# Graph attention with residual and layer norm: whole tiles of keys and queries in turns of two and one, scale found ahead of DVE's copies, ends reordered

## The reference

```
q = x @ Wq.T          k = x @ Wk.T          v = x @ Wv.T + bv
scores = einsum(q, k) * 384**-0.5 + 2 * adj          # per head, 128 x 128
scores = where(any(scores != 0 in the row), scores, -inf)
p = nan_to_num(softmax(scores))
out = einsum(p, v) @ Wo.T + bo
result = layernorm(x + out)
```

## Time and profile before

| | us |
|---|---|
| median of 3 runs | 605.71 |
| lowest and highest | 602.56, 606.85 |
| the profiled execution | 605.91 |
| its span | 604.1 |
| PE busy | 581.2 (96%) |
| ACT busy | 497.4 (82%) |
| DVE busy | 492.9 (82%) |
| POOL busy | 425.2 (70%) |
| mean granted clock of TensorE | 0.996 |

### The profile page before, as it was taken

One profiled execution on the slowest core, in us unless ns is written; L12 is line 12 of the kernel. 1 busy time (PEld: TensorE's weight loads), 2 busy tenths in 40 slices (PEclk: granted clock), 3 DMA queues, 4 the chain that ended last, 5 costly groups with the idle time before them and its releaser, 6 DMA issues.

```text
span 604.1 us, 23413 instructions
## 1 busy us (share of the span) xinstructions
PE 581.2 (96%) x8448; PEld 511.6 (85%) x8448; DVE 492.9 (82%) x2380; ACT 497.4 (82%) x1975; POOL 425.2 (70%) x691
## 2 busy tenths in 40 slices
PE   8889999999999999999999999999999999999776
PEld 5678888889988988888888988988888888898665
DVE  4568888888888888878887887888888888888886
ACT  5598888888887988978888887988988888887883
POOL 0476867867776876867867776876867777665763
PEclk9899999999999999999999999999999999999999
DMA  8401422414242241432323242241423231222221
GB/s 298 164 17 37 131 92 67 141 60 126 92 129 87 70 131 57 139 90 88 113 69 118 91 131 90 65 135 53 142 91 104 91 92 53 84 91 81 89 83 67
DMA packets 34748, 59.62 MB, mean 99 GB/s; under 512 B 10568, under 2 KB 24008, under 8 KB 34632
## 3 DMA queue, kind: packets, MB, share of 16 engines
q1 hardware_dynamic: 34200, 57.53, 30.0%
q10 hardware_dynamic: 432, 0.59, 0.3%
HBM read 44.50 MB, written 13.62 MB: 96 GB/s over the span
## 4 chain that ended last, share of the span: by engine, by line
PE 69%; DMA 11%; ACT 9%; DVE 4%; SPq 1%; issue 1%; POOL 0%; POOLq 0%; DVEq 0%
PE qk_ps L343 25%; PE scores_ps L441 12%; PE v_ps L379 11%; PE scores_ps L366 7%; ACT probs L491 7%; PE scores_ps L424 6%; PE qk_ps L396 6%; DMA scale_mem<-scale_rows 6%; DMA scale_t<-scale_mem 6%; DVE nscores L591 2%; DVE att_n L661 1%; ACT out_n L530 1%; SPq L252 1%; PE spare_ps L396 1%; SPq L248 0%
## 5 line engine op out<-in xcount | busy, mean ns | idle before, releaser
L491 ACT ACTIVATE probs<-nscores,neg_max 128x128 f32<-128x128 f32 x768 | 297.4, 389 | 13.3 <-DVE neg_max L591 9.0
L591 DVE CUSTOM_DVE_ANT_0 nscores<-scores_ps,adj_n 128x128 f32<-128x128 f32 x768 | 171.4, 285 | 29.1 <-PE scores_ps L366 27.1
L289 POOL TENSOR_TENSOR tree<-nscores 128x256 f32<-128x256 f32 x192 | 144.0, 750 | 18.9 <-DVE neg_max L591 18.9
L491 ACT ACTIVATION_READ_ACCUMULATOR probs<-nscores,neg_max 128x1 f32 x768 | 144.2, 188 | 0.0
L517 ACT ACTIVATE probs_t<-qk_ps 128x384 f32<-128x384 f32 (+1 forms) x128 | 63.1, 493 | 77.4 <-PE spare_ps L396 74.4
L441 PE MATMUL scores_ps<-w_o,att_t 128*128 128x384 f32 x576 | 112.3, 339 | 5.4 <-DVE probs_t L616 4.9
L379 PE MATMUL v_ps<-w_v,x_t 128*128 128x384 f32 x576 | 111.4, 338 | 3.5 <-ACT probs_t L517 3.5
L289 POOL TENSOR_TENSOR tree<-tree 128x128 f32<-128x128 f32 x192 | 101.3, 527 | 15.0
L379 PEld LDWEIGHTS v_ps<-w_v,x_t 128*128 128x128 f32 x576 | 101.7, 188 | 9.7 <-ACT probs_t L517 4.3
L343 PE MATMUL qk_ps<-x_t,w_q 128*128 128x512 f32 (+1 forms) x540 | 107.2, 343 | 0.7 <-ACT probs_t L517 0.7
L343 PE MATMUL qk_ps<-x_t,w_k 128*128 128x512 f32 (+1 forms) x540 | 107.8, 344 | 0.0
(11 more groups left out here) (71 smaller groups left out, 946.9 us busy)
## 6 DMA issues: line engine op xcount, KB each, us to landing
x_n<-xn SPq DMA_DIRECT2D x32, 384.0 KB, 5.1
scale_t<-scale_mem SPq DMA_DIRECT2D x63, 192.0 KB
out<-out_n SPq DMA_DIRECT2D x31, 384.0 KB, 2.6
x_raw<-xt SPq DMA_DIRECT2D x15, 768.0 KB, 5.5
adj_n<-adj SPq DMA_DIRECT2D x32, 128.0 KB, 4.6
scale_mem<-scale_rows SPq DMA_DIRECT2D x63, 16.0 KB
x_raw<-xt SPq DMA_DIRECT2D x3, 256.0 KB, 6.0
nscores<-wq ACTq DMA_DIRECT2D x3, 192.0 KB, 4.1
```

The source lines that it names most:

```text
L289: nc.gpsimd.tensor_tensor(tree[:, b % 2, low:high, 0:width], src[:, :, 0:width], src[:, :, width:2 * width], ALU.add).then_inc(tree_step, 1)
L491: last = nc.scalar.activation(probs[:, b % 2, h], nscores[:, b % 2, h], ACT.Exp, bias=neg_max[:, b % 2, h:h + 1], scale=-1.0, accum_out=ro ...
L591: last = nc.vector.tensor_tensor_reduce(out=nscores[:, half, h], in0=scores_ps[j][:, m * P:(m + 1) * P], in1=adj_n[:, b // 2 % 2, half], s ...
```

## The change

Tiles: `projected(b)` gives two whole tiles in even slots and one in odd slots. The second of the two goes to `qk_ps[1]` with 512 columns and is copied by ACT as a whole; in odd slots ACT copies nothing. Semaphore values follow (`second_tiles`).

DVE: `find_scale(b + 1)` comes right behind the biases and ahead of `keep_turned_high`, `keep_first` and `keep_v`.

PE: `project_out` waits for the biases of graph b + 2 (as the argument counts, `biased >= KT * (b + 4)`) in place of the copy `turned_high`. `attend` waits for `turned_high` always, and for ACT's copies in slots with fewer than two tiles.

Start: the low part of w_o moves on DVE from before the copies of the first queries into slot -2, and its high part on ACT behind the copies of the first keys; `softmax_top` of graphs 0 and 1 waits for the split weights, whose raw form lies in the same buffers.

End: POOL adds the bias rows of graphs 62 and 63 in slot 61; ACT copies the bank of `v_ps` first in the last two turns.

```
         def projected(b):
             ...
             if b % 2 == 0:
-                return (tile, 0, GRP * P), (tile + 1, 0, GRP * P // 2)
-            return (tile + 2, 0, GRP * P), (tile + 1, GRP * P // 2, GRP * P)
+                return tile, tile + 1
+            return (tile + 2,)
+
+        def second_tiles(b):
+            return (slots_with_tiles(b) + 1) // 2
# POOL
-                if has(b):
+                if 0 <= b < NB - 2:
                     add_bias(b)
+                if b == NB - 3:
+                    add_bias(NB - 2)
+                    add_bias(NB - 1)
# PE
             def project(b, n, tile):
                 ...
                 elif b == -1:
-                    pe.wait_ge((kept_first, kept_second)[n], 1)
+                    pe.wait_ge(kept_first, 1)
                 ...
-                        last = nc.tensor.matmul(qk_ps[n][:, start:end], w[:, a, k, cols], x_t[:, g % XBUFS, c, k, start:end],
+                        last = nc.tensor.matmul(qk_ps[n][:], w[:, a, k, cols], x_t[:, g % XBUFS, c, k],
             def values(b):
-                    pe.wait_ge(turned_low, LOWS * (b - 1) + 2)
+                    pe.wait_ge(turned_low, LOWS * (b - 1) + (2 if has(b + 1) else 1))
             def turn(b):
-                if b == 0:
-                    pe.wait_ge(kept_second, slots_with_tiles(b - 1))
-                elif not projected(b - 1):
+                if projected(b - 1):
+                    pe.wait_ge(kept_second, second_tiles(b - 1))
+                else:
                     pe.wait_ge(probs_ready, KT * (b + 1))
             def attend(b):
-                if projected(b):
-                    pe.wait_ge(kept_second, slots_with_tiles(b))
-                    if b == 0:
-                        pe.wait_ge(turned_high, 1)
-                else:
+                pe.wait_ge(turned_high, b + 1)
+                if len(projected(b)) < 2:
                     pe.wait_ge(turned_low, LOWS * (b + 1))
-                    pe.wait_ge(turned_high, b + 1)
             def project_out(b):
                 if has(b + 3):
-                    pe.wait_ge(turned_high, b + 2)
+                    pe.wait_ge(biased, KT * (b + 4))
# ACT
             def softmax_top(b, m):
                 ...
+                    if b < 2:
+                        act.wait_ge(w_split, b + 1)
             def keep_second(b):
-                act.wait_ge(proj_done, 2 * b + 6)
+                act.wait_ge(proj_done, tile + 1)
                 ...
-                nc.scalar.activation(dst[:, g % 2, t % KT, start:end], qk_ps[1][:, start:end], ACT.Copy,
-                                     scale=scale).then_inc(kept_second, 1)
+                nc.scalar.activation(dst[:, g % 2, t % KT], qk_ps[1][:], ACT.Copy, scale=scale).then_inc(kept_second, 1)
             ...
-            act.wait_ge(wo_in, DMA)
-            nc.scalar.activation(w_o[:, HI], raw_o, ACT.Copy).then_inc(w_high, 1)
             for m in range(KT):
                 act.wait_ge(first_done, 2 * m + 1)
                 nc.scalar.activation(k_t[:, 0, m], first_ps[2 * m][:], ACT.Copy).then_inc(first_keys, 1)
-            act.wait_ge(w_split, 2)
+            act.wait_ge(wo_in, DMA)
+            nc.scalar.activation(w_o[:, HI], raw_o, ACT.Copy).then_inc(w_high, 1)
             for b in range(-2, NB - 2):
                 ...
-                if b == -1:
-                    keep_second(b)
                 softmax_top(b + 2, 2)
-                if projected(b) and b != -1:
+                if len(projected(b)) > 1:
                     keep_second(b)
             ...
-            keep_turned_low(NB - 2, 0, LOWS)
+            keep_turned_low(NB - 2, 1, 0, 2)
             attention_high(NB - 3)
-            keep_turned_low(NB - 1, 0, LOWS)
+            keep_turned_low(NB - 1, 0, 1, 2)
# DVE
-            for n, (w, raw) in enumerate(((w_v, raw_v), (w_o, raw_o))):
+            def split_w_low(n, w, raw):
                 dve.wait_ge(w_high, n + 1)
                 nc.vector.tensor_tensor(w[:, LO], raw, w[:, HI].bitcast(F32), ALU.subtract).then_inc(w_split, 1)
+            split_w_low(0, w_v, raw_v)
             ...
                 bias_and_max(b + 2, 2)
+                if has(b + 1):
+                    find_scale(b + 1)
                 if has(b):
                     keep_turned_high(b)
                 if projected(b):
                     keep_first(b)
+                if b == -2:
+                    split_w_low(1, w_o, raw_o)
                 if has(b + 1):
                     keep_v(b + 1)
-                    find_scale(b + 1)
```

More of the change, by code:

```diff
@@ L326, in run_idle, with project @@
                     nc.tensor.matmul(bank[:], zeros[:, 0:P], zeros[:], start=True, stop=True)
-            def project(b, n, tile, start, end):
+            def project(b, n, tile):
                 g, t = tile // TILES + 1, tile % TILES
@@ L462, in _ @@
                 score(b + 2)
-                for n, (tile, start, end) in enumerate(projected(b)):
-                    project(b, n, tile, start, end)
+                for n, tile in enumerate(projected(b)):
+                    project(b, n, tile)
                     if n == 0 and has(b + 1):
@@ L496, in keep_second @@
             def keep_second(b):
-                tile, start, end = projected(b)[1]
+                tile = projected(b)[1]
                 g, t = tile // TILES + 1, tile % TILES
-                act.wait_ge(proj_done, 2 * b + 6)
+                act.wait_ge(proj_done, tile + 1)
                 wait(act, scores_done, (g - 1) * GRP)
                 dst, scale = ((k_t, 1.0), (q_t, 0.5 * SCALE))[t // KT]
-                nc.scalar.activation(dst[:, g % 2, t % KT, start:end], qk_ps[1][:, start:end], ACT.Copy,
-                                     scale=scale).then_inc(kept_second, 1)
+                nc.scalar.activation(dst[:, g % 2, t % KT], qk_ps[1][:], ACT.Copy, scale=scale).then_inc(kept_second, 1)
             def split_x_high(g, k):
@@ L510, in split_x_high, with keep_turned_low @@
                 nc.scalar.activation(x_t[:, g % XBUFS, HI, k], x_raw[:, g % 2, k], ACT.Copy).then_inc(x_high, 1)
-            def keep_turned_low(b, first, end):
-                if first == 0:
-                    act.wait_ge(turned, b + 1)
-                    wait(act, pv_done, b)
-                for j in range(first, end):
+            def keep_turned_low(b, *banks):
+                act.wait_ge(turned, b + 1)
+                wait(act, pv_done, b)
+                for j in banks:
                     nc.scalar.activation(turned_rows(b, j), turned_bank(b, j), ACT.Copy).then_inc(turned_low, 1)
@@ L548, in _ @@
                 nc.scalar.activation(k_t[:, 0, m], first_ps[2 * m][:], ACT.Copy).then_inc(first_keys, 1)
-            act.wait_ge(w_split, 2)
+            act.wait_ge(wo_in, DMA)
+            nc.scalar.activation(w_o[:, HI], raw_o, ACT.Copy).then_inc(w_high, 1)
             for b in range(-2, NB - 2):
                 if has(b):
-                    keep_turned_low(b, 0, 1)
+                    keep_turned_low(b, 0)
                 if has(b - 1):
@@ L556, in _ @@
                 if has(b):
-                    keep_turned_low(b, 1, LOWS)
+                    keep_turned_low(b, 1, 2)
                 softmax_top(b + 2, 0)
                 softmax_top(b + 2, 1)
-                if b == -1:
-                    keep_second(b)
                 softmax_top(b + 2, 2)
-                if projected(b) and b != -1:
+                if len(projected(b)) > 1:
                     keep_second(b)
@@ L602, in keep_first @@
             def keep_first(b):
-                tile = projected(b)[0][0]
+                tile = projected(b)[0]
                 g, t = tile // TILES + 1, tile % TILES
-                dve.wait_ge(proj_done, 2 * b + 5)
+                dve.wait_ge(proj_done, tile + 1)
                 wait(dve, scores_done, (g - 1) * GRP)
```

## The result

| | before | after |
|---|---|---|
| median of 9 runs each | 604.18 | 607.18 |
| lowest and highest | 602.56, 606.85 | 605.53, 607.99 |
| the profiled execution | 605.91 | 607.18 |
| its span | 604.1 | 605.4 |

The ratio is 1.005 with a 95% interval of 1.003 to 1.0069: the change made the kernel 3.0 us slower, where 2.3 us faster was forecast. The time lies in the range, on the other side of no change. The two profiled executions differ by 1.3 only, because the one of before came out 1.7 above its median.

A forecast was written before the change was run, and what follows sets the result against it. PE was taken as the bound, busy 99 of 100 us. Terms -0.2 + 3.5 - 1.9 - 2.2 - 1.5 = -2.3 take the profiled 605.91 to 603.6 us; the 8 in 10 range is 599.5 to 609.

The forecast's parts named there:

- Tiles: PE's projections in the loop: two whole tiles and one by turns remove 270 matmuls, -0.2 us for all.
- The lag on DVE: Odd slots: DVE's normalisation comes later and delays score by 0.12 us in each of 29 pairs, +3.5 us.
- rival 2: DVE's loop becomes the odd slot's bound, 7.96 against PE's 7.87; at 0.35 a pair 610.3 us; chance 0.14.
- turning point of 0.20 a pair: The lag per pair of slots from which rival 2 decides, only 0.08 above the forecast's figure.
- bound of 0.35: Upper bound of DVE's lag per pair, 10.2 us, if the transpose holds the next copy and the scale's waits grow.
- The scales' DMA: Seven waits of normalisation for the scales: ACT without the half copy issues transfers 0.27 earlier each, -1.9 us.
- the bound of -3.4: Lower bound of the scales' DMA term, in us, if all seven waits vanish.
- Start: Kernel start: w_o split moved, full clock, shorter softmax chain, less a larger tile in slot 0; -2.2 us.
- End: Four slots without tiles: output projection waits for biases, slots near 7.5, and POOL's last bias row earlier; -1.5 us.
- signs that I had set for being wrong: Even slots longer than 10.2, turns waiting for v, or the clock falling at the start all the same.

The follow-up runs named there:

- Experiment 2: Changed kernel with the scale found one place later on DVE, right behind the copy of the turned probabilities: 599.80 us, ratio 0.9934 to the kernel before.
- 3: Changed kernel with the old tiles (one and a half in each slot), scale still early: 600.62 us, ratio 0.994 to the kernel before.
- 4: Changed kernel with the old tiles and the scale found late, behind keeping v: 600.07 us, ratio 0.9933 to the kernel before.
- 5: Changed kernel plus an unused addition of 192 columns on DVE behind the residual of odd slots: 616.15 us, ratio 1.0212 to the kernel before.
- 10: Changed kernel with the old tiles and the scale right behind the turned copy: 600.23 us, ratio 0.9951 to the kernel before.
- 1: Changed kernel with whole tiles kept, but the scale found behind keeping v as before: 605.39 us, ratio 1.0031 to the kernel before.
- Experiment 8: Changed kernel with the scale behind the turned copy, but the first scale behind keeping v: 600.85 us, ratio 0.996 to the kernel before.
- 12: Changed kernel with old tiles, scale behind the turned copy, and SP issuing store and x load behind the next scale: 596.62 us, ratio 0.99.
- experiment 6: Changed kernel plus an unused addition of 192 columns on DVE behind the residual of even slots: 628.03 us, ratio 1.0411 to the kernel before.
- 7: Changed kernel with the low part of the attention moved on DVE between the last biases and the scale: 613.75 us, ratio 1.0173.
- 9: Changed kernel plus the addition of 192 columns in even slots, one input from PSUM instead of both from SBUF: 607.98 us, ratio 1.0077.

## Why the prediction was wrong

The terms between the two profiled executions: start, loop and end changed by -0.96, +2.57 and -0.34, together +1.27. The start does half a tile (1.05) more and the loop half a tile less, so at equal work they are -2.0 and +3.6. Measured against the forecast of -2.3, the lag is 3.6 us more, the end 1.2, the start and the tiles 0.2 each, and the scales' DMA 1.6 less. The medians lie 1.7 further apart, since the forecast started from an execution 1.7 above the median of nine.

1. **Tiles, -0.2 forecast.** Right: nothing is won (6.48 against 6.50 a pair). The Trainium skill's fixed cost for each matmul, quoted in the prediction, would have given an estimated 0.7 in all, 0.02 a pair; rows given to 0.01 us can't tell that from nothing.
2. **The lag on DVE, +3.5 forecast; this is the step that failed.** It measured +7.1 (29 odd slots of 7.95 and 28 even ones of 10.14 make 514.5, against 507.4 for 7.87 and 9.97). The mechanism was the one named: in odd slots DVE's loop ends in the normalisation that score waits for. The size was off because I took the place "behind the biases" to cost what "behind keeping v" cost, 1.20 to the transpose, and priced only the transpose's neighbour behind it (0.14, right). The reduction waits for all biases; with v in front of it that wait was long over, with the last bias in front it is 0.18. The loop that rival 2 adds up, 7.96, is 8.12 as measured, and that is the 0.18 less some hundredths elsewhere. (By that sum the forecast itself should have had 0.09 a pair and not 0.12.) Experiment 2 took the 0.18 away by a swap (0.19 a pair, 4.85 net in the loop), 3 and 4 showed that slots of 8.92 don't feel it, and 5 that an odd slot passes on everything that is added. The prediction's rival 2 had the mechanism and its turning point of 0.20 a pair, and gave it 0.14. Its bound of 0.35 held. Against it stood "every other neighbour on DVE starts before its forerunner ends", and that misread the trace: inside the scale, where each instruction waits for the result of the one in front, the next one starts 0.03 to 0.10 behind its forerunner's end. In the kernel before:

```profile
310.43 0.22 DVE L630 RECIPROCAL recip<-row_sum 128x12 f32<-128x12 f32 x1
310.75 0.18 DVE L643 SCALAR_TENSOR_TENSOR row_scale<-scores_ps,recip 128x12 f32<-128x12 f32 x1
```

A reading of 0.08 and such a 0.10 behind it are the 0.18.
3. **The scales' DMA, -1.9 forecast.** It measured -3.5: all seven waits went, the bound of -3.4. The prediction put it down to ACT alone and said that the earlier scale buys nothing there. The runs, one execution each, speak against that: with the old tiles five to seven waits stay, wherever the scale stands (3.8 us in 3, 3.3 in 10, 3.2 in 4), and with whole tiles they are 3.0 us with the scale late (1), 1.0 behind the turned copy (2) and none behind the biases. Part of this may be the lag itself, which makes the deadline later; no run tests that apart.
4. **Start, -2.2 forecast.** -2.0 measured, and that it fits is luck. The wait shrank by 1.59 and score(0) ran at full clock, 0.7 less, as forecast. Three things were in no step. The tiles of slot -2 had run at half clock too, and gained another 0.7. The turn's wait for v behind the first scale cost 0.9. And in slot 0 a tile at half clock cost 1.3, where two waits of 0.65 for ACT's copies fell away. Experiment 8 shows that the wait for v is only the first of several that ACT's copies set.
5. **End, -1.5 forecast.** -0.3 measured. I worked with the wait of output projection alone, and did not carry "the scale ahead of the turned copy" into the slots without tiles, where DVE has no slack: attention waits there, and the slots 58 and 59 are longer still (7.86 and 7.91). The four slots gave 0.7 where 1.35 was forecast. And the wait of graph 62 for its scale grew from 0.64 to 1.57, which made the last stretch 0.7 longer; that was in no step either. With the turned copy first the slots are the 7.5 that I expected (2, 4), and the issue order of 12 takes the wait away.

Two of the signs that I had set for being wrong came: turns wait for v, and the clock fell at the start.

## What to carry to other kernels

Before a consumer of several results is moved directly behind the last of its producers on the same engine, look for the time from the producer's end of turn to its result: in the old place other work may have covered it. Splitting work unevenly over slots cost nothing here on the engine that does it, and took the room from the engine whose work stayed even; check such a loop against the short slot, with its waits, to the hundredth. And on a queue in order, try to issue what has a deadline ahead of what waits for another engine or moves a large block.

## What the runs showed of the hardware

An addition of 192 columns on DVE with both inputs in SBUF took 1.22 us beside POOL's split of x and ended 0.21 after it; with one input in PSUM it took 0.35 beside the same split, and with both in SBUF and no POOL instruction in its way 0.35 too (the last three of experiment 6, and all but the last of 5, where none of POOL's ran at its start). The split of the attention (384 columns, both inputs in SBUF) took 0.96 beside POOL's sum and ended 0.41 after it, where it takes 0.56 at its old place in most slots. (In the change 13 of the 64 take some 0.75, and they end 0.40 after one of POOL's too.) The 0.21 and 0.41 are in proportion to the 192 and 384 columns, so such an instruction seems to do its work only after POOL's has ended. It goes the other way as well: in experiment 5 a split of POOL's that started 0.02 after such an addition took 1.47 instead of 1.28. The Trainium skill ("SBUF — State Buffer", section "Who interferes with whom") states that a DVE instruction with two inputs in SBUF contends with a GpSimd instruction that reads SBUF, and that the port pair which the two engines share is an exclusive lock. Experiments 6, 7 and 9 agree.

The granted clock after the wait at the start is not settled by the program. In the profiled executions of the change and of experiment 5, whose starts have the same order, the idle time before the first turn is the same 1.42; in the change the clock went to 0.50 behind it, in 5 it stayed at full:

```profile
34.00:35.00 1.00, 0.94 (x4) 0.82 (x5) 1.00 (x9) 0.83 (x4) 1.00 (x1) 1.00 0.19 52
```

The tile of slot 0 took 3.47 in the one and 2.19 in the other, and slot 1 started at 41.95 and at 40.84. The nine executions of the change differ in the same way among themselves: seven have a mean granted clock of 0.995 or 0.996, the fastest (605.53) has 0.999. That is over 1 us from one execution to the next, over a third of the 3.0 between the two kernels, and a reason to compare medians.
